# Expert rows of five early groups: turned on TensorE and copied by SP instead of scattered by GpSimd

## What is computed

```python
xn = (x - mu) * rsqrt(var + EPS) * gamma + beta
logits = xn @ Wr + br
top_vals, top_idx = top_k(logits, 2)
w = softmax(top_vals)
for e in range(8):
    h = gelu(xn @ W1[e] + b1[e])
    y += (h @ W2[e] + b2[e]) * w_full[..., e, None]
```

## Time and profile before

| what | value |
|---|---|
| median of three runs | 2605.71 us (2603.78 to 2613.53) |
| span of the profiled execution | 2600.8 us |
| busy: POOL, DVE, PE, ACT | 1853.9, 1559.2, 1557.1, 693.4 us |
| L1088, gathers | 1612, 1574.7 us busy |
| L287, scatters | 98, 101.9 us busy |
| mean granted TensorE clock | 0.675 of full speed |

### The profile page before, as it was taken

The page is one execution under the profiler, slowest core; times in us unless marked ns, Lnnn a source line. Parts: engine busy times, 40 slices in busy tenths (PEclk is TensorE's granted clock), DMA queues, the critical chain, the costliest instruction groups (busy, mean ns, idle before and its releaser), DMA issues. The chain is left out here.

```text
span 2600.8 us, 54069 instructions
## 1 busy us (share of the span) xinstructions
PE 1557.1 (60%) x17407; PEld 1202.7 (46%) x17407; DVE 1559.2 (60%) x5736; ACT 693.4 (27%) x2061; POOL 1853.9 (71%) x1870
## 2 busy tenths in 40 slices
PE   6666666556666535425434764765666475648893
PEld 4444444535444324323323653544555354537782
DVE  7677776667777655545545665565666656544333
ACT  6422221112222132022113323324322433322220
POOL 2476667777777777777777777777777777755673
PEclk9777786655556555555555866766777677778997
DMA  7355556734555454454455666466666666557886
GB/s 212 99 150 158 154 157 167 208 106 129 164 153 155 139 161 108 108 161 110 109 146 166 176 181 202 140 183 177 178 179 201 182 182 189 163 171 206 241 231 197
DMA packets 286477, 429.03 MB, mean 165 GB/s; under 512 B 72790, under 2 KB 214312, under 8 KB 286060
## 3 DMA queue, kind: packets, MB, share of 16 engines
q0 software_dynamic: 94320, 246.50, 34.8%
q1 hardware_dynamic: 182748, 170.53, 21.7%
q10 hardware_dynamic: 9120, 8.48, 1.0%
HBM read 348.54 MB, written 72.13 MB: 162 GB/s over the span
## 5 line engine op out<-in xcount | busy, mean ns | idle before, releaser
L1088 POOL DMA_INDIRECT region<-node_table,src_idx x1612 | 1574.7, 977 | 588.3 <-issue 467.3
L1291 PE MATMUL ps_p<-region 128*32 128x65 f32 x12896 | 391.3, 289 | 455.1 <-DVE region L1555 454.1
L1291 PEld LDWEIGHTS ps_p<-region 128*32 128x32 f32 x12896 | 302.8, 151 | 555.0 <-DVE region L1555 548.8
L1162 ACT ACTIVATE ps_p<-region 128x16 f32<-128x16 f32 x403 | 75.4, 187 | 1289.8 <-DVE region L1549 1289.3
L1273 PE MATMUL ps_s<-ident,region 128*128 128x128 f32 x403 | 166.6, 414 | 418.1 <-DVE region L1549 411.0
L1563 DVE SCALAR_TENSOR_TENSOR acc<-ps_p,region,acc 128x65 f32 x806 | 192.8, 280 | 291.1 <-issue 285.5
L1555 DVE TENSOR_TENSOR region<-region,ps_p 128x512 f32<-128x512 f32 x403 | 273.4, 678 | 51.9 <-ACT ps_p L1162 50.9
L1273 PEld LDWEIGHTS ps_s<-ident,region 128*128 128x128 f32 x403 | 87.3, 217 | 449.1 <-DVE region L1549 441.7
L1277 PEld LDWEIGHTS ps_s<-region 128*128 128x128 f32 x806 | 195.8, 274 | 58.6 <-issue 32.5
L1547 DVE TENSOR_TENSOR region<-region,ps_s 128x16 f32<-128x16 f32 x403 | 67.9, 169 | 235.4 <-DMA region<-node_table,src_idx 205.5
L1158 ACT ACTIVATE region<-ps_s 128x128 f32<-128x128 f32 x403 | 111.0, 276 | 288.8 <-PE ps_s L1273 287.4
(11 more groups left out here) (347 smaller groups left out, 2634.4 us busy)
## 6 DMA issues: line engine op xcount, KB each, us to landing
region<-in_W_dram SPq DMA_DIRECT2D x84, 512.0 KB, 5.7
region<-node_table,src_idx POOLq DMA_INDIRECT x1612
acc<-in_W_dram SPq DMA_DIRECT2D x28, 512.0 KB
region<-expert_in SPq DMA_DIRECT2D x47, 258.0 KB, 5.9
acc<-base_rows SPq DMA_DIRECT2D x13, 896.0 KB, 6.2
qkv_rows<-region SPq DMA_DIRECT2D x49, 194.0 KB
y_rows<-acc SPq DMA_DIRECT2D x28, 256.0 KB
node_table<-region SPq DMA_DIRECT2D x49, 132.0 KB, 1.7
```

The lines of the kernel that those rows point to most:

```text
L1088: pool.indirect_dma_start(out=rows[:, s, j, :], out_offset=None, in_=table[:, :], in_offset=bass.IndirectOffsetOnAxis(ap=src_idx[:, n * SU ...
L1291: m = pe.matmul(ps_p[s % 2][h * WIN:(h + 1) * WIN, 0:HC], wts[:, s % 2, j, h, :], rows[:, s, j, h * HC:(h + 1) * HC], start=j == 0, stop=j ...
```

## The change

The 35 tiles of groups 0 to 4 (`TURNED = 5`) are no longer scattered by GpSimd. For each tile DVE builds a 128 by 256 selection matrix from the row's place among the tile's 256 sent rows sorted by expert, PE multiplies it with the rows in two products, ACT copies both out of PSUM (`ps[3]`) to `sorted_rows`, and SP stores the 256 sorted rows to a DRAM table `run_rows`, waits for that store, and copies eight runs, one for each expert, from `run_rows` to `expert_in`, each always 128 rows long. Rows beyond the run are overwritten by what comes later, so the copies of a tile wait for those of the tile before. The turning is at steps u = 33 to 48, the steps of SP at u = 37 to 50; steps from 39 on lie in the blocks of the next group. A row in `expert_in` is 260 words instead of 258, since one sorted row carries both gates and its first expert, and the gate is chosen when the expert tile is worked off (`weigh_rows`). `sent_rows` is written once instead of twice. Carried tiles come three blocks later (`CARRY_AT` 10 to 13).

```diff
-MROW = DIM + 2
+MROW = DIM + 4
+TURNED = 5
+TURN_U = 33
+SLOT = 5 * P
...
         elif u == 8:
-            if r.k:
+            if r.m:
+                turned.wait(sp, 2 * r.m)
+            if r.s:
                 sp.wait_ge(sent, 32 * r.s)
             sp.sem_inc(ring_free, 1)
...
+        elif r.turned and u >= TURN_U + 4 and (u - TURN_U - 4) // 2 < n:
+            j = (u - TURN_U - 4) // 2
+            m = r.m + j
+            if (u - TURN_U - 4) % 2 == 0:
+                turned_out.wait(sp, 2 * (m + 1))
+                if m:
+                    run_out.wait(sp, RUNS * m)
+                sp.dma_start(run_rows[j * SLOT:j * SLOT + 2 * P, :].rearrange("(c p) d -> p c d", p=P),
+                             sorted_rows[:, m % 2]).then_inc(run_in.sem, 16)
+            else:
+                run_in.wait(sp, 16 * (m + 1))
+                send_runs(sp, j)
...
+    def send_runs(sp, j):
+        for e in range(E):
+            v = sp.value_load(run_at[0:1, j * E + e:j * E + e + 1], min_val=0, max_val=N_PAD * 512 + 511)
+            to = expert_in[e * CAP:(e + 1) * CAP, :][bass.ds(v >> 9, P), :]
+            sp.dma_start(to.rearrange("(a b) c -> a (b c)", a=16),
+                         run_rows[j * SLOT:(j + 1) * SLOT, :][bass.ds(v & 511, P), :].rearrange("(a b) c -> a (b c)", a=16)).then_inc(run_out.sem, 16)
...
-            act.activation(sent_rows[:, j, :, 0:DIM], bcast(x_all[:, j, :], 1, 2), ACT.Identity,
+            act.activation(sent_rows[:, j, 0:DIM], x_all[:, j, :], ACT.Identity,
...
+            if m >= 2 and c == 0:
+                run_in.wait(act, 16 * (m - 1))
+            act.activation(sorted_rows[:, m % 2, c, :], ps[3][:, 0:MROW], ACT.Copy).then_inc(turned_out.sem, 1)
...
+            pe.matmul(ps[3][:, 0:MROW], sel[:, m % 2, c * P:(c + 1) * P], sent_rows[:, j, :], start=True, stop=True).then_inc(turned.sem, 1)
...
+            own.do(dve.tensor_scalar(sel[:, m % 2, :], spot[:, :], spots[:, 0, j:j + 1], None, ALU.is_equal))
+            dve.scalar_tensor_tensor(out=sel[:, m % 2, :], in0=spot[:, :], scalar=spots[:, 1, j:j + 1], in1=sel[:, m % 2, :],
+                                     op0=ALU.is_equal, op1=ALU.add).then_inc(chosen.sem, 1)
...
+def weigh_rows(dve, own, gates, choice, expert):
+
+    own.wait()
+    own.do(dve.scalar_tensor_tensor(out=gates, in0=choice[:, :, 0], scalar=expert, in1=choice[:, :, 2], op0=ALU.is_equal, op1=ALU.mult))
+    own.step(dve.tensor_tensor(gates, gates, choice[:, :, 1], ALU.add))
...
-    def sync(sp, m, sent_count):
+    def sync(sp, m, tiles):
         q, s = m // CARRY, m % 2
         listed.wait(sp, q + 1)
-        sp.wait_ge(sent, sent_count)
+        run_out.wait(sp, RUNS * tiles)
...
-    CARRY_AT, CARRY_STEP = 10, 5
+    CARRY_AT, CARRY_STEP = 13, 5
...
-    for k in range(EARLY - 2):
-        for j in range(SIZES[k]):
-            SENDS.setdefault(STARTS[k + 1] + j, []).append((k, j))
```

More of the change, by code:

```diff
@@ L204 @@
 EARLY_TILES = sum(SIZES[:EARLY])
-MAIN_SENT = sum(SIZES[:EARLY - 1])
+MAIN_TURNED = sum(SIZES[:TURNED])
+MAIN_SENT = sum(SIZES[TURNED:EARLY - 1])
+RUNS = 16 * EXPERTS
 EARLY_PAIRS = pairs_in(SIZES[:EARLY])
@@ L294, in send @@
             pool.wait_ge(routed, r.k + 1)
+            if r.m:
+                run_out.wait(pool, RUNS * r.m)
             pool.sem_inc(ticks, 1)
@@ L302, in pair, with turn, turn_half @@
         return range(j, min(r.gt, j + 2)) if u >= start and (u - start) % 4 == 0 else ()
+    def turn(r, u, d):
+        k = u - TURN_U - d
+        return k // 2 if r.turned and 0 <= k < 2 * r.gt and k % 2 == 0 else None
+    def turn_half(r, u, d):
+        k = u - TURN_U - d
+        return divmod(k, 2) if r.turned and 0 <= k < 2 * r.gt else None
     def pair_end(j, r):
@@ L341, in scalar @@
             act.activation(t1_all[:, 0:n], t1_all[:, 0:n], ACT.Exp).then_inc(exp_out, 1)
+        j = turn_half(r, u, 2)
+        if j is not None:
+            j, c = j
+            m = r.m + j
+            turned.wait(act, 2 * m + c + 1)
+            if m >= 2 and c == 0:
+                run_in.wait(act, 16 * (m - 1))
+            act.activation(sorted_rows[:, m % 2, c, :], ps[3][:, 0:MROW], ACT.Copy).then_inc(turned_out.sem, 1)
     part.scalar = scalar
@@ L353, in tensor @@
             pe.wait_ge(n_ready, r.t + (j + 1))
+            if j == 0 and r.m:
+                turned_out.wait(pe, 2 * r.m)
             if j >= 2:
@@ L415, in vector @@
             pick(dve, own, n, lg, 0, first)
+            own.do(dve.tensor_copy(sent_rows[:, 0:n, DIM + 1], gate))
         elif u == 30:
@@ L672, in vector @@
             i.then_inc(xeT_ready.sem, 1)
+            weigh_rows(dve, own, gates[:, m % 4, :], choice[:, m % 4], b1s[:, m % 4, FC:])
         elif v == 8:
@@ L708, in main_stage @@
     FREE_FROM += (-FREE_FROM) % SL
-    CARRY_AT, CARRY_STEP = 10, 5
+    CARRY_AT, CARRY_STEP = 13, 5
     STARTS = [FREE_FROM + d for d in (0, 39, 78, 118, 157, 197)]
-    STEPS = {s + u: [(k, u)] for k, s in reversed(list(enumerate(STARTS))) for u in range(ROWS_U)}
+    STEPS = {}
+    for k, s in enumerate(STARTS):
+        for u in range(TURN_U + 4 + 2 * GT if k < TURNED else ROWS_U):
+            STEPS.setdefault(s + u, []).append((k, u))
     QUICK = STARTS[-1] + 33
@@ L1031, in _ @@
                 if n == FIRST_AT:
[L1032 removed]
+                    carried.first_tiles(sp, 1)
             for i in range(2):
@@ L1383, in _ @@
                     carry_sems["listed"].wait(pe, LISTED)
+                    part.turned_out.wait(pe, 2 * MAIN_TURNED)
                     send_notes(g, pe, ps_x[3], noted_ps)
@@ L1671, in rows_constants @@
                     own.step(dve.memset(done[:, :], 0.0))
+                    own.step(dve.tensor_copy(spot[:, :], spot[:, :].bitcast(I32)))
                 elif n == 2:
@@ L1849, in round_of @@
                     part.sums(sp, early_round(k, 1))
-                    for u in range(ROWS_U):
+                    for u in range(TURN_U + 4 + 2 * GT):
                         part.sync(sp, early_round(k, 1), u)
@@ L1875, in rest @@
             def rest():
-                for k in range(EARLY - 1):
+                for k in range(TURNED, EARLY - 1):
                     for j in range(SIZES[k]):
@@ L2278, in rows_back @@
                 m.then_inc(xeT_ready, 1)
+                weigh_rows(dve, own, gates[:, n % MS, :], choice[:, n % MS], b1s[:, n % MS, FC:])
             def result(n):
```

136 lines of the change are left out of this document (92 added, 44 removed).

## The result

| what | before | after |
|---|---|---|
| median of four runs beside each other | 2604.74 us (2596.77 to 2613.53) | 2813.05 us (2809.74 to 2815.86) |
| ratio | | 1.080, interval 1.077 to 1.082 |
| span of the profiled execution | 2600.8 us | 2807.7 us |

The change costs 208 us. The forecast was a loss of 105 (2710), so the loss is twice as large. 2813 lies 7 us inside the upper end of the forecast's own case (2630 to 2820) and 12 us inside the whole range (2550 to 2825).

The account below looks back on a forecast made before the run. POOL was taken to bound, with SP's serial tiles becoming the path: span 2600.8 + 109 - 10 + 6 - 1 = 2705, time 2710 us. Own case 2630 to 2820 (chance 0.57), whole range 2550 to 2825.

Parts of the forecast that it names:

- What bounds, and the relief of 91 us: POOL sets the pace in the changed stretch; removing 35 tiles' scatters at 2.60 us each frees 91 us.
- The work added to DVE, PE and ACT: Sorting work per tile: DVE passes about 1.0 us, two PE products about 0.41 each, two ACT copies 0.37 each.
- One copy, 1.25 us: SP's register load and issue for one run: 1.25 us, bounds 1.15 and 1.60; eight take 10.0 us.
- Rival 3: Register loads on SP are slow among the copies, 1.60 us a copy: +78 us on four ways, 2788 us; chance 0.09.
- Store and landing: SP's waits per tile: store 3.7 us plus 0.1 wake-up, landing of the last copy 3.1 us.
- The tile, 16.9 us, and seven tiles: SP's series per tile takes 16.9 us (13.7 to 22.1); seven tiles take 118 us instead of 70.
- The way, 137 us: From step 36's L1547 to the next group's step 15: 137 us; four ways 548 instead of 439, so +109.
- Group 0, -10: No carried tile follows group 0; POOL ends 10 us ahead and the following blocks keep this.
- Steps 15 to 36, +6: In groups 2 to 4, about 6 us of new DVE work against some 4 of waits: +6 us together.
- Neutral at 13 us a tile: The change neither gains nor loses when SP takes about 13 us a tile.
- That SP keeps up: SP takes under 13 us a tile and DVE bounds: -52 us, 2554 us; chance 0.17.
- That traffic delays the gathers: The 280 copies delay gathers, each tile costing a 3 us wait: another 84 us, 2794 us; chance 0.05.

Follow-up runs that it names:

- the early store: The changed kernel, but SP stores each tile before copying the tile before it, with copy landings counted on two semaphores: 2720.92 us, ratio 1.043.
- the run with group 0 alone: Changed kernel with each tile's store ahead of the previous tile's copies, only group 0 sorted, groups 1 to 4 scattered by GpSimd: 3001.30 us, ratio 0.9976.

## Why the prediction was right in kind and short in size

The mechanism was right: SP's series over a tile, and PE waiting behind it. The size was half of what was measured, and that 2813 still lies in the range is luck in part: 12 us more, and it would not.

**What bounds, and the relief of 91 us:** right. With cheap stores in the scatters' place the gain was 101 us where blocks are some 15% longer.

**The work added to DVE, PE and ACT:** right in effect. DVE's two passes took 0.86 us a tile, forecast 1.0. PE's product took 0.65 us in the mean instead of 0.41: the row comes from the tail, where TensorE's granted clock is 0.83 to 0.97 of full speed, and group 0's tiles run at 0.50. The waits cover it.

**One copy, 1.25 us:** mis-sized. It measured 1.58, eight 12.6 instead of 10.0: the issue is 0.53 us, not 0.38, and the load's own register operations are 0.15. The forecast's bound of 1.60 held for the quiet tiles (the median of all is 1.62), its choice inside the bounds did not; it took the lower of the two ACT rows. Rival 3 had the price and nearly the time (2788), but for another reason: it put the price down to slow register loads, and these were as quick as before (268 ns).

**Store and landing:** right in sum. 3.2 us of wait against 3.7, 2.1 against 3.1 for the last copy. They give back 1.5 of the 2.6 us that the copies cost more.

**The tile, 16.9 us, and seven tiles:** the shortest interval of each group measured 17.2 to 18.2, the median of the groups' last three 18.2. From first to last store the forecast had 6 x 16.9 + 9.0 + 0.4 = 111 us. Measured were 121, 129, 127 and 129, together 63 us more. SP's neighbours in the list have a part in it: in groups 2 to 4 the first interval is 23 to 24 us, and the third up to 23.5. The second, with the next group's row loads, is 28 to 28.5 in groups 1 to 4, where the forecast had 25.9. In group 2's third stands a carried tile (timeline of SP), whose load and weights go out between a store and its copies; the copies start 9.4 us after their store instead of some 4. The forecast had no carried tile in any interval.

```profile
1633.10 0.50 SPq L306 DMA_DIRECT2D run_rows<-acc  x1
1634.54 0.39 SPq L698 DMA_DIRECT2D region<-expert_in  x1
...
1636.88 0.80 SPq L703 DMA_DIRECT2D acc<-in_b_dram  x1
1642.51 12.13 SPq L317 DMA_DIRECT2D expert_in<-run_rows  x8
```

**The way, 137 us:** measured 146, 160, 159 and 163, in all +189 instead of +109. This is the term that failed in size; 63 of the missing 80 us are the intervals above. Most of the rest stands ahead of them: the first store comes 1.9 us after the L1656 of step 36 in group 1, about as forecast (1.7), but 7.8, 7.8 and 8.2 us after it in groups 2 to 4, 19 us in all. There a carried tile's load and weights are issued right ahead of the store (L698 at 1579.74, 1855.85 and 2129.39), and the store's own copies start 8.6 to 10.4 us after it instead of some 4. Behind the last store the ways are as forecast (23.2 to 25.2 us against 24.6).

**Where the time is lost:** half told. The waits for `xe` came as said, four of them, but 104.5 us are not the whole loss. ACT's wait for the store two tiles back, which the forecast priced for group 0 alone, stopped PE 145.3 us in all, 24 to 35 in every group. POOL stood for PE 56 to 84 us from each of the steps 36 of groups 1 to 4 to the next, where the forecast had some 30. It is the same delay of SP, met by PE earlier, which decides what helps. Moving the carried tiles away from the copies gave 37 us, taking the store's landing out of the series 94.

**Group 0, -10:** not borne out; the loop was 4.9 us late after it. With the early store it was 5.8 us ahead, so the sign of the forecast hung on SP's waits for landings; PE stood 23.8 us for ACT's copy-out there, up to 16.7 at once, more than the reserve of 14 us.

**Steps 15 to 36, +6:** 2.5, 2.1 and 1.3 us in groups 2 to 4, as said. From group 5's step 15 on: +8.1 instead of -1. POOL stood for PE 28.4 us in the first 21 of these blocks, which I read as the rest of a lag that the reserve was to have absorbed.

**Neutral at 13 us a tile:** about right for this order of SP, by a rough sum. Of a way of 157 us after, 126.6 are the six intervals of groups 1 to 4; with the other 30 unchanged, the 110 us of before leave 80 / 6 = 13.3 us for a mean interval, the row loads among them.

**Rivals.** That SP keeps up failed (17.6 us a tile). That traffic delays the gathers has little for it. With the same bytes copied at fixed addresses the kernel gained. DVE also waited only 26.7 us for gathers in group 1's blocks after, 61.0 in the earlier trace rows; that is the weaker sign, since a DVE that is late finds its gathers landed. The `tensor_load` floor of about 600 ns that the Trainium skill gives in "DMA: Bandwidth & Descriptors" (section "Latency and other measured facts") is not seen on SP in either kernel: 268 ns is the median of 280.

```profile
DVE region L1656 <- DMA region<-node_table,src_idx: 26.7, 19, 3.2
```

**Still open:** what the bytes alone cost on the usual chip, since fixed addresses were only run in the slower sets; what the rest of a dynamic copy (shift, mask, two computed addresses) costs beside the unread load, since no set has both; and whether a version with four of seven tiles sorted would beat both kernels. It was not tried.

## What to carry to other kernels

Before work moves to a "free" queue, add up that queue's instructions in issue time, each register load, shift and issue, and set the sum against the period of the loop: here 280 dynamic copies of 1.58 us stood against 35 steps of 10 us. Taking the landings out of the series gave back 94 of the 208 us, but with the sum over the period the kernel stayed 4% slower; with the sum under it, in kernels that leave the right places out, it was up to 3% faster. Add up the queue's other entries too: carried loads beside the stores made a good part of what the forecast lacked. The sorting, multiplying and copying of the other engines was nearly free, working out an address in registers was not.

## What the hardware showed beyond that

- On SP an address in a register costs what comes before the issue, not the issue. A load to SBUF with a dynamic address is issued in 0.38 us, a store from SBUF at fixed addresses in 0.40 (median of L306). A copy from DRAM to DRAM takes 0.53 with two dynamic addresses and 0.59 with fixed ones. Eight such copies are issued in 4.9 us at fixed addresses, in 8.2 to 11.4 with one unread load before each (both in the slower sets), and in 11.5 to 12.2 with load and two computed addresses on the usual chip.
- The same kernel before took 2607.74, 2971.47 and 3008.56 us in three sets of runs. The record numbers the chip 2 in the first set and 1 in the other two, so whether the last two are one chip at two times is not known. SP's register work is slower there too: in the run with group 0 alone, eight copies took 14.2 to 18.7 us. A ratio taken in one set is not that of another: 95 us of intervals gave 1.043 on the usual chip, 109 us gave 1.000 in a slower set.
- What an fp32 product takes goes by the granted clock, more than by four more columns. The sorting product (260 columns) takes 641 to 804 ns in group 0, where the clock is 0.50 of full speed (1.2 GHz), first line; the tail's product of 256 columns in the kernel before takes 379 in the median from 2402 to 2498 us, where it is 0.96 (2.4 GHz most of the time), second line. Where a sorting product meets the full clock, as at 2218.7 us, it takes 383.

```profile
L431 PE MATMUL ps_x<-acc x28: 641/722/804, 1085.1 to 1180.8; 128*128 128x260 f32 x28
...
L2232 PE MATMUL ps_eu<-region x192: 377/379/763, 2403.1 to 2497.6; 128*128 128x256 f32 x192
```
